# Splitting the steps of a hand-ordered program by engine, folding a convolution into its input product, and one weight transfer per expert

## The reference

```python
x = x + attn(ln(x))     # "A": linear attention, 16 heads of 8, a decayed state scanned over time
x = x + moe0(ln(x))     # "B": 8 experts, top 2, hidden 352: silu(x W1) * (x W3), times W2
x = x + ssm(ln(x))      # "C": u = x Win + b_in; depthwise conv of 3 taps over time; silu;
                        #      selective scan with 16 states; gate; Wout
x = x + moe1(ln(x))     # "D": 8 experts, top 2, hidden 128, and 2 shared experts
```

## Time and profile before

| | us |
|---|---|
| median of 3 runs | 2368.11 |
| the three runs | 2198.21, 2368.11, 5253.03 |
| the profiled execution | 2195.7 |
| its span, first to last instruction | 2193.9 |
| busy: PE / DVE / ACT / POOL | 1546.3 / 1436.8 / 1084.5 / 897.8 |
| mean granted clock of TensorE | 0.833 |

### The profile page before, as it was taken

How to read it: one execution, slowest core, us unless ns; L and a number is a source line. 1 busy time by engine, 2 the same in 40 slices (tenths; PEclk the granted TensorE clock), 3 DMA queues, 4 the chain that set the end, 5 groups by cost and what they waited for, 6 DMA issues and landing times.

```text
span 2193.9 us, 31883 instructions
## 1 busy us (share of the span) xinstructions
PE 1546.3 (70%) x9792; PEld 997.2 (45%) x9792; DVE 1436.8 (65%) x2710; ACT 1084.5 (49%) x1998; POOL 897.8 (41%) x599
## 2 busy tenths in 40 slices
PE   4548668778788676788688766777789667555771
PEld 1226446435465454435455544435455555222541
DVE  4845658778777465888786465977797338668610
ACT  2143365458553674448453574447554565253541
POOL 0130520363227743444237644272246660733065
PEclk8769779888899898888899687987899789767786
DMA  9357359436765597536856586636775589437463
GB/s 244 56 152 208 67 167 313 150 79 221 248 200 154 138 300 222 152 80 207 292 149 163 136 266 206 191 68 191 249 226 148 146 205 338 128 98 245 121 155 77
DMA packets 342098, 392.45 MB, mean 179 GB/s; under 512 B 37768, under 2 KB 279464, under 8 KB 341672
## 3 DMA queue, kind: packets, MB, share of 16 engines
q1 hardware_dynamic: 296872, 356.70, 52.6%
q0 software_dynamic: 45056, 33.72, 8.6%
HBM read 332.57 MB, written 59.16 MB: 179 GB/s over the span
## 4 chain that ended last, share of the span: by engine, by line
issue 26%; POOL 20%; PE 18%; DMA 15%; ACT 10%; DVE 6%; SPq 5%; POOLq 1%; ACTq 0%; DVEq 0%
POOL x L740 11%; DMA mix<-weights 5%; POOL rows_D L723 4%; PE bank L907 3%; POOL rows_B L723 3%; DMA x<-outs,slot_idx 3%; PE bank L762 2%; DMA rows_D<-xrow,slot_idx 2%; DMA outs<-yrow 2%; ACT xn L993 2%; PE bank L764 2%; PE bank L763 2%; SPq L620 1%; PE bank L838 1%; DMA rows_B<-xrow,slot_idx 1%
## 5 line engine op out<-in xcount | busy, mean ns | idle before, releaser
L740 POOL DMA_INDIRECT x<-outs,slot_idx x256 | 492.7, 1924 | 566.1 <-DMA outs<-yrow 378.0
L762 PE MATMUL bank<-xT_ring,mix 128*128 128x128 f16 (+1 forms) x1536 | 321.3, 241 | 125.2 <-DMA mix<-weights 93.8
L763 PE MATMUL bank<-xT_ring,mix 128*128 128x128 f16 (+1 forms) x1536 | 319.2, 240 | 0.0
L764 PE MATMUL bank<-xT_ring,mix 128*128 128x128 f16 (+1 forms) x1536 | 319.0, 240 | 0.0
L838 PE MATMUL bank<-arena_c,ident 128*128 128x512 f32 x512 | 260.5, 645 | 52.3 <-DVE arena_c L1325 52.0
L1339 DVE TENSOR_TENSOR_SCAN arena_c<-arena_c 128x1024 f32<-128x1024 f32 x128 | 289.0, 2276 | 3.7 <-ACT arena_c L1082 3.2
L907 PE MATMUL bank<-mix 128*128 128x128 f32 (+1 forms) x1536 | 235.3, 300 | 61.5 <-DVE mix L1451 28.2
L907 PEld LDWEIGHTS bank<-mix 128*128 128x128 f32 (+1 forms) x1536 | 207.2, 207 | 104.6 <-DVE mix L1451 63.5
L762 PEld LDWEIGHTS bank<-xT_ring,mix 128*128 128x128 f16 (+1 forms) x1536 | 178.6, 116 | 166.6 <-DMA mix<-weights 110.5
L1451 DVE SCALAR_TENSOR_TENSOR mix<-bank,winv,mix 96x256 f32<-96x256 f32 (+1 forms) x192 | 90.9, 479 | 150.0 <-ACT mix L1123 138.2
L723 POOL DMA_INDIRECT rows_D<-xrow,slot_idx x128 | 166.9, 1304 | 46.7 <-issue 33.8
(11 more groups left out here) (209 smaller groups left out, 2844.6 us busy)
## 6 DMA issues: line engine op xcount, KB each, us to landing
arena_c<-bc_rows SPq DMA_DIRECT2D x256, 512.0 KB, 6.8
mix<-weights_B SPq DMA_DIRECT2D x192, 352.0 KB
mix<-weights SPq DMA_DIRECT2D x192, 192.0 KB
outs<-yrow SPq DMA_DIRECT2D x192, 128.0 KB, 3.9
mix<-weights_D SPq DMA_DIRECT2D x192, 128.0 KB
xg<-rows_B SPq DMA_DIRECT2D x96, 129.0 KB, 4.4
xg<-rows_D SPq DMA_DIRECT2D x96, 129.0 KB, 2.7
mix<-in_W SPq DMA_DIRECT2D x192, 64.0 KB
```

The lines of the kernel that those rows point to most:

```text
L740: pool.indirect_dma_start(out=x[:, b % XS, j, :], out_offset=None, in_=y_d[q], in_offset=bass.IndirectOffsetOnAxis(ap=slot_idx[:, q % RJ, ...
L762: pe.matmul(o, hi, xh, start=True, stop=False)
L763: pe.matmul(o, hi, xl, start=False, stop=False)
L764: return pe.matmul(o, lo, xh, start=False, stop=True)
```

## The change

1. **Steps are split by engine.** `b_a` becomes `b_a` (TensorE, letter U) and `b_a_silu` (ScalarE, L); `b_b_gate` and `b_c_gate` (VectorE) are letter V; `b_turned` M; `b_down_read` Y; `b_out_read` Z; `sh_add` a; `a_carry` k. The fronts A, C and P stay one chain each with more steps in it (`s_turn` and `s_turned`, `c_in` and `c_read`, `m_logits`, `m_centre`, `m_exp`, `m_rank`). The banks get 13 counters of emptying in place of 8, so that a reader waits for its own kind alone.
2. **The convolution is folded into the product.** Once, `Wconv[i] = Win * w_i` for three taps (two small instruction groups and one TensorE product) and three bias columns. Then `u` is three accumulated products per half, the side taps shifted by a column, and ScalarE applies silu straight from the bank, with one extra column for the edge. `c_conv` on VectorE and the read of `u` on ScalarE are gone.
3. **One weight transfer per half.** W1, W3 and W2 of an expert lie in one DRAM row and one buffer; a block takes two transfers, not four. For D the room falls from six blocks of W2 to five.
4. **A new `ORDER`** of 5579 steps. The order of jobs is the same.

```diff
-            steps += [("c_in", b, "u", h) for h in range(NH)] + [("c_conv", b)]
-            steps += [("c_in", b, "z", h) for h in range(NH)] + [("c_xs", b)]
+            steps += [(m, b, n, h) for n in "uz" for m in ("c_in", "c_read") for h in range(NH)]
...
+            "M": [("b_turned", q, k) for q in range(len(JOBS)) for k in range(BLOCKS)],
             "U": [st for q in range(len(JOBS)) for st in ups(q)],
+            "L": [st for q in range(len(JOBS)) for st in silus(q)],
+            "V": [st for q in range(len(JOBS)) for st in gates(q)],
...
                 if k >= RW[s]:
-                    U.wait_filled(wt, f"c{q}.{k - RW[s]}")
-                if k >= R2[s]:
-                    U.wait_filled(wt, f"y{q}.{k - R2[s]}")
+                    U.wait_filled(wt, f"y{q}.{k - RW[s]}")
                 for i in range(NBT):
...
-                    sp.dma_start(w13(s, k, i).rearrange("p w f -> p (w f)"),
+                    sp.dma_start(expert_weights(s, k, i),
                                  Wd[s][bass.ds(e, 1), :, :].rearrange("o p f -> p (o f)")).then_inc(w_in[m % RWL], 16)
-                    sp.dma_start(w2(s, k, i).rearrange("p c d -> p (c d)"),
-                                 W2d[s][bass.ds(e, 1), :, :].rearrange("o p f -> p (o f)")).then_inc(w_in[m % RWL], 16)
...
+                first, last = int(h == 0), int(h == NH - 1)
+                pe.matmul(o, Wconv[:, 1, :], half(normC, h), start=True, stop=False)
+                pe.matmul(o[:, first:HW], Wconv[:, 0, :], normC[:, h * HW + first - 1:(h + 1) * HW - 1], start=False, stop=False)
+                filled(n, pe.matmul(o[:, 0:HW - last], Wconv[:, 2, :], normC[:, h * HW + 1:(h + 1) * HW + 1 - last],
+                                    start=False, stop=True))
...
+                    act.activation(half(xs, h)[:, inner], o[:, inner], ACT.Silu, bias=conv_bias[:, 2:3])
+                    read(n, act.activation(half(xs, h)[:, edge:edge + 1], o[:, edge:edge + 1], ACT.Silu, bias=conv_bias[:, h:h + 1]))
...
-                dve.tensor_scalar(conv, u_in, convw[:, 1:2], col["convb"], ALU.mult,
-                                  ALU.add).then_inc(c_conv.sem, 1)
-                for i, to, of in ((0, slice(1, T), slice(0, T - 1)), (2, slice(0, T - 1), slice(1, T))):
-                    wt.wait_ge(c_conv.sem, c_conv.at(b, 1 + i // 2))
-                    dve.scalar_tensor_tensor(out=conv[:, to], in0=u_in[:, of], scalar=convw[:, i:i + 1], in1=conv[:, to],
-                                             op0=ALU.mult, op1=ALU.add).then_inc(c_conv.sem, 1)
```

More of the change, by code:

```diff
@@ L81 @@
[L81 to L95, removed]
@@ L249, in build @@
         dt, w, z = (arena_c[:, at + i * T:at + (i + 1) * T] for i in range(3))
-        normC, u_in, conv, xs = (hb[:, i, :] for i in range(4))
+        normC, xs = hb[:, 0, :], hb[:, 3, :]
+        taps = hb[:, 1, 0:3 * D].rearrange("p (i d) -> p i d", d=D)
         sp_abs, sp_log, bc_f = dA[:, 0, :], dA[:, 1, :], dA[0:BC, 2, :]
@@ L334, in prepare @@
         def prepare(q):
[L335 to L336 removed]
+            return ([("m_stats", q), ("m_rstd", q), ("m_shift", q)] + [("m_norm", q, h) for h in range(NH)] +
+                    [(n, q, h) for h in range(NH) for n in ("m_turn", "m_turned")] + [("m_hi", q), ("m_rows", q)] +
+                    [("m_logits", q), ("m_centre", q), ("m_exp", q)] + [("m_lo", q)] * (JOBS[q][0] == "D") +
+                    [("m_choose", q), ("m_rank", q), ("m_place", q)] +
                     [("m_scatter", q, i) for i in range(PARTS)])
@@ L344, in ups, with silus, gates @@
             return shared(q, "sh_up", NH * SH) + [(n, q, k) for k in range(BLOCKS) for n in names]
+        def silus(q):
+            names = ("b_a_silu", "b_c_silu") if JOBS[q][0] == "B" else ("b_c_silu",)
+            return shared(q, "sh_silu", NH * SH) + [(n, q, k) for k in range(BLOCKS) for n in names]
+        def gates(q):
+            names = ("b_b_gate", "b_c_gate") if JOBS[q][0] == "B" else ("b_c_gate",)
+            return shared(q, "sh_gate", NH * SH) + [(n, q, k) for k in range(BLOCKS) for n in names]
         def combine(q):
@@ L820, in c_in, with conv_weights @@
                 U.wait_empty(wt, f"C{b}.ln{h}")
-                filled(n, pe.matmul(fill(n), {"u": Win, "z": Wz}[name][:], half(normC, h), start=True, stop=True))
+                o = fill(n)
+                if name == "z":
+                    filled(n, pe.matmul(o, Wz[:], half(normC, h), start=True, stop=True))
+                    return
+                U.wait_empty(wt, "taps")
+                U.wait_empty(wt, f"C{b}.ln{NH - 1}")
+                first, last = int(h == 0), int(h == NH - 1)
[3 more added lines that the diff above has]
+                                    start=False, stop=True))
+            def conv_weights():
+                wt.wait_ge(s_cons, 7)
+                wt.wait_ge(conv_ready, 3)
+                o = fill("taps", 3 * D)
+                filled("taps", pe.matmul(o, ones[:], taps.rearrange("p i d -> p (i d)"), start=True, stop=True))
             def c_dt(b, h):
                 n = f"C{b}.dt{h}"
-                wt.wait_ge(xs_done.sem, xs_done.at(b, 1))
+                U.wait_empty(wt, f"C{b}.u{h}")
                 filled(n, pe.matmul(fill(n), Wdt[:], half(xs, h), start=True, stop=True))
```

240 lines of the change are left out of this document (145 added, 95 removed).

## The result

The change makes the kernel slower by about 1.7%, where the prediction had it 9% faster.

A forecast was written before the change was run, and what follows sets the result against it. No engine was the bound: stages full of VectorE work alternated with stages where a job's latency ran alone. Order 156, transfers 20 and convolution 16 us off 2193.9 gave 2002 us of span, 2004 in all; range 1900 to 2150.

The forecast's parts named there:

- Start to job 2: First three stages: attention moved into VectorE's half-idle time, job 2's first block at 483 us, gain 8 us.
- to turn work into time I divide by 0.85: Stage lengths: VectorE's work in a stage divided by a busy share of 0.85, with ends 0.80 and 0.90.
- 80 us between jobs 0 and 1 is possible once job 1 is scattered before job 0 is gathered: Stage from job 0 to 1: could take 80 us, as job 0's twelve blocks took 68.2 us.
- Stages 3 to 4, 7 to 8, 11 to 12: Stages ending in a D job: shortened to 84, 100 and 100 us, gains of 41, 34 and 40 us.
- until C's gate, plus 67 us: Stages ending in a D job: last until C's gate, then 67 us to D's first block.
- rival A: B stages do not shrink because the block loop sets them, moved attention was hidden; 133 us lost, 2137 us, chance 0.21.
- Stages 2 to 3, 9 to 10, and behind job 13: Loss of 9 us to 91, gain of 18 to 187, and gain of 24 from finer steps behind job 13.
- The stages left as they were: Stages 4 to 7, 8 to 9, 10 to 11, 12 to 13 and the last 84.9 us: no change claimed.
- Part 2: Weight loads, one transfer instead of two: TensorE's waits for weights shrink, 20 us gained, between 0 and 35.
- Part 3: Convolution folded into TensorE's product: 2 us a batch on the way to C's scans, 16 us, ends 0 and 36.
- B: Five separate ScalarE reading steps in each of 192 blocks wait in its queue, 1.5 us a block: 2292 us, chance 0.11.
- C: Attention put first delays jobs 0 and 1, VectorE reaching only 0.64: all 153 us later, 2157 us, chance 0.06.

The follow-up runs named there:

- e10: Changed kernel with the new order up to job 0's first block and the old order behind it; 2244.1 us beside 2225.3 for before.
- e11: Kernel before with VectorE's attention triples on 16 of their 512 columns; 2195.8 us, 0.987 of before.
- e8: Changed kernel with VectorE's attention triples on 16 of 512 columns; 2248.1 us, 1.009 of before.
- e14: e10 with job 1's preparation and scatter and batch 2's attention front moved in among job 0's blocks; 2241.2 us beside 2193.1 for before.
- e6: Changed kernel with the old order up to job 12's first block and the new one behind it; 0.991 of before.
- e2: Kernel before with the single weight transfer alone, in old order with old convolution; 0.994 of before.
- e1: Changed kernel with all its code changes but the old order, split steps side by side; 0.997 of before.
- e5: Changed kernel with the new order up to job 2's first block and the old order behind it; 2278 us, 1.020 of before.
- e7: Changed kernel with one weight load per block instead of two and room for four blocks of weights; 2221.5 us, 0.997 of before.
- e12: e10 with job 1's preparation and scatter moved in among job 0's blocks; 2210.0 us beside 2193.1 for before.

## Why the prediction was wrong, point by point

**The state of things before.** "No engine is the bound" and "something must be late again and again" stood. The step that followed was wrong: VectorE's idle share in the first 302 us (58% and 50% busy) was read as room. In the stage from job 0 to 1 it is time in which VectorE waits for other engines: 147 to 150 us long with VectorE 39, 47 or 76 us busy (e10, e11, before).

**Start to job 2: 483 us forecast, 561 measured.** This is the first failed step: "to turn work into time I divide by 0.85". The shares came out as 72%, 62% and 80%, 74% up to job 2, where the prediction's sign was above 80%. e11 shows that 29 us less of VectorE's work moves the stage from job 0 to 1 by nothing. The start does answer to it, but not at 1 / 0.85 = 1.18 us for each us of work: 35 us less of work gave 24 us (e11), 59 less gave 26 (e8), and 35 more, with 16 triples moved in, cost 20 (e10). GpSimd stands there with nothing to do until VectorE has job 0's places, and scatters from 138.0 us, where before it did from 108.2. On GpSimd, in order of time:

```profile
136.58 0.46 POOL L753 COPY xrow<-gate 128x8 f32<-128x8 f32 x1 [29.31 <-DVE slot_idx L1488]
137.99 2.00 POOL L756 DMA_INDIRECT rows_B<-xrow,slot_idx  x1 [0.94 <-POOL xrow L753]
```

The forecast of 153 us for the start came out as 172. Beside job 1, 247 came out as 281, the one stage at about the share that it had before (80%). There the sum took too little work as well: 210.0 us forecast, 225.1 measured, since norms and fronts of other batches came in with the triples.

"80 us between jobs 0 and 1 is possible once job 1 is scattered before job 0 is gathered" measured the wrong thing: it came to 107, and job 1 is not on the way to D0. To have job 1's rows ready early, its preparation must pass all queues among job 0's blocks, and job 0's blocks are on the way. The prediction counted what is moved as triples of VectorE, and left out the 51 other steps that the new order moves, 25 of the 70 us by e14.

**Stages 3 to 4, 7 to 8, 11 to 12: 84, 100 and 100 us forecast, 116, 127 and 131 measured.** This is the second failed step, and the larger one: "until C's gate, plus 67 us". The gates did move forward: those of C1, C3 and C5 come 10, 42 and 50 us after the first block of their B job, where they came 58, 67 and 73 us after it. But D's first block followed them by 106, 85 and 81 us, and 67 was no rule; before, D6 already took 105. The traces show where the 67 us grew (before and after, us):

| | gate to the end of D's scatter | to the load of its first rows | to its first block |
|---|---|---|---|
| D1 | 62.0, 82.8 | 1.7, 15.0 | 3.3, 8.1 |
| D3 | 62.3, 69.4 | 1.4, 6.2 | 3.0, 9.5 |
| D5 | 61.3, 64.9 | 1.8, 4.4 | 4.0, 11.3 |

For D1 the first two columns show queues at work. GpSimd stops in the middle of the scatter for a norm step of attention that the new order puts there and that is not ready, and SyncE has stores of job 3's blocks ahead of D1's rows. On GpSimd and SyncE:

```profile
714.11 1.67 POOL L739 TENSOR_TENSOR rstd_A<-ve_A,neg_half 128x8 f32<-128x8 f32 x1 [17.31 <-DVE ve_A L1274]
735.58 0.97 POOL L756 DMA_INDIRECT rows_D<-xrow,slot_idx  x1 [0.30 <-issue]
751.54 0.47 SPq L666 DMA_DIRECT2D xg<-rows_D  x1
```

So a second path ends close to the gate's, the B job's own twelve blocks: 103, 102 and 103 us from first to last, and D's first block comes 12, 25 and 28 us behind the last of these. It is the later one in the first of the three stages, and within some 6 us of the gate's in the others. Before, the rows were loaded right behind the scatter, so the gate's path alone ended last, and I saw only that one. The forecast also asked too much of TensorE: it is busy 90.8, 99.0 and 96.6 us of these stages, so 84 us was less than its own work in one, and 100 asked for 97 to 99% in the others. The row that could have told it was in the earlier trace rows (107.7 of 134.0), and the prediction cites it for rival A. In the first of the three it was 108.0 us, against a forecast of 84. The floor of 84.6 us from job 13 was the one of job 13's own stage, with other work beside it.

**Stages 2 to 3, 9 to 10, and behind job 13.** 83 us where 91 was forecast; 202 where 187 was, by the same divided sum; 332 for the two stages behind job 13 where 320 was. That gain, 12 of the 24 us, is the part of the order that e6 confirms.

**The stages left as they were.** Between jobs 2 and 12 these (4 to 7, 8 to 9, 10 to 11) cost 18 us together where the prediction had nothing: 4 to 5 and 5 to 6 are 12 and 25 us longer, 8 to 9 is 15 shorter. No run takes them apart.

**Part 2, 20 us.** It measured 13 (e2), inside its ends of 0 and 35; the mechanism was given as the waits of TensorE, and the traces do not bear it out: 93.8 us before, 89.3 in e2, 80.8 in e1, 97.1 after, where 20 less were forecast. So that the size came out is in part luck. With the single buffer SyncE waits longer for the room of the weights, behind the down product: 254 us before, 322 in e2, 374 after. The Trainium skill (DMA: Bandwidth & Descriptors, "Anatomy of one DMA") has a fixed cost near 2.0 us a transfer. It gives it for transfers that GpSimd issues, and these are SyncE's. The prediction's estimate from it was 70 us; 384 transfers fewer gave 13 us in all, and by the earlier trace rows they are issued back to back, so that they can overlap.

**Part 3, 16 us.** Nothing that can be told: e1 and e2 differ by 0.3% the other way. The 27 us of VectorE went, as read from the earlier trace rows, but the way to the gate of C0 is as long as it was, so for that batch they were not on the path. The folded version was not run by itself, so its share stays open.

**The table loads.** 143 against 133, ten more as counted, 13 us of ScalarE, and the 51 loads of L1131 again had 0.9 us of idle time before them in all.

```profile
L1131 ACT ACT_TABLE_LOAD x51 | 65.4, 1283 | 0.9
```

The Trainium skill (ScalarE: Activation LUTs, "What ACT_TABLE_LOAD costs") would have about 1.38 us of drain at each. Here too no row shows it. Not every load is hidden, though. ScalarE was idle 40.1 us before the 28 loads of L1165, nearly all of it waiting for TensorE's products (L797). The load comes only once the product is there, and its 1.28 us then stand in the block's own path to silu. So it was before (L1116, 30 loads, 37.9 us). What the ten more loads cost, no run tells.

**The rivals.** A, "the moved attention was hidden anyway", is most of what happened behind job 2 (e5): the four stages gave 29 of the 133 us. Weights, the first thing that A named in the block loop, do not set it (e7). Its 2137 us still carried the gain of the first stages. B's price, 1.2 us and more in each block from the split itself, did not come: with the same split steps in the old order job 0's blocks take 67 us (e1). Its sign, job 0's blocks well above 68 us, did come with the new order (101), from what the order puts between the steps. That is close to B's mechanism, a step of a block behind other work in a queue, in one job; e12 to e14 do not tell ScalarE's queue from the others. C had the right place and half of its size, 78 of 153 us against the forecast, but named VectorE's share as the cause. A and C were treated as cases that exclude each other. Both came. The 241 us are C's 78, 104 of A's 133, the 36 of parts 2 and 3, 18 in the stages left as they were and 13 behind job 12, less 8 from job 2 to 3. That is why the range, which reached only up to each rival by itself, did not hold the time.

## What to carry to other kernels

Where every engine runs its steps in one written order, do not turn an engine's work into time by a busy share. Write down the chain of jobs that ends the stage (here blocks, gather, C, gate, next job), and for every step that the new order puts among that chain's steps ask which queues it passes and what work it brings there, triples or not. Work brought forward into idle slots is free only off that chain, and pays only where no second chain (here the B job's own blocks, and TensorE's own work in the stage) ends at the same time. When a forecast shortens a stage, divide each engine's busy time by the new length before believing it.

## What the runs showed of the hardware

When VectorE's triples and TensorE's sums of them became narrow, TensorE's granted clock fell on the mean from 0.846 to 0.809 (e8) and from 0.833 to 0.808 (e11; the seven runs of before beside it had 0.824 to 0.833). The engine was busy 38 and 57 us less, and was granted less. Part of what e8 and e11 could have won may have been lost so; how much, no run here tells apart.
